# Layer 0 and 1 of a four-layer graph stack: when rows of adj are prepared, which comes first of roots, counts and fills, and how often adj is widened

## The reference, cut to what matters

```
L0:  deg = adj.T.sum(1); y = (d^-1/2 * adj.T * d^-1/2) @ (h @ W0) + b0
L1:  head = (adj > 0); head = head / max(sqrt(row sum of head^2), 1e-12)
     inc = adj + head; y = (inc @ h) / inc.sum(-1)
L2:  four heads: e = leaky_relu(src_i + dst_j) + adj; y = mean over heads of softmax(e) @ (h @ W2)
L3:  y = relu(adj @ (max(sign(h), 0) @ sign(W3).T))
```

## Time and profile before

| | us |
|---|---|
| median of three runs | 729.1 |
| the profiled execution | 732.13, span 730.2 |
| TensorE busy | 691.9 (95%) |
| VectorE busy | 629.2 (86%) |
| ScalarE busy | 480.3 (66%) |
| GpSimd busy | 106.9 (15%) |
| mean granted TensorE clock | 0.991 |

### The profile page before, as it was taken

The page is one execution under the profiler, slowest core; times in us unless marked ns, Lnnn a source line. Parts: engine busy times, 40 slices in busy tenths (PEclk is TensorE's granted clock), DMA queues, the critical chain, the costliest instruction groups (busy, mean ns, idle before and its releaser), DMA issues.

```text
span 730.2 us, 16136 instructions
## 1 busy us (share of the span) xinstructions
PE 691.9 (95%) x6480; PEld 585.0 (80%) x6480; DVE 629.2 (86%) x1165; ACT 480.3 (66%) x830; POOL 106.9 (15%) x146
## 2 busy tenths in 40 slices
PE   2898999996999999999999999999999899999998
PEld 2665888885888885458888888888888788888887
DVE  5887579788989864799999999989999799998683
ACT  3997162739987723886557867578766778667661
POOL 3002721211223220001210021200120100000000
PEclk9998999998999999999999999999999999999999
DMA  9886999868499976759988779897999931126791
GB/s 330 315 293 234 413 423 330 238 145 210 162 275 270 210 172 222 163 118 246 241 189 239 175 162 264 191 265 163 228 220 218 310 92 30 30 68 195 250 387 54
DMA packets 146458, 159.55 MB, mean 218 GB/s; under 512 B 90896, under 2 KB 103888, under 8 KB 141904
## 3 DMA queue, kind: packets, MB, share of 16 engines
q1 hardware_dynamic: 127328, 117.10, 54.4%
q0 software_dynamic: 19056, 41.42, 25.2%
HBM read 76.15 MB, written 52.46 MB: 176 GB/s over the span
## 4 chain that ended last, share of the span: by engine, by line
PE 55%; DVE 20%; ACT 10%; POOL 5%; issue 5%; DMA 4%; SPq 2%; ACTq 0%; POOLq 0%; DVEq 0%
PE ps L829 12%; PE ps L831 12%; PE ps L830 12%; PE ps L769 6%; DVE arena L1486 5%; DVE arena L1493 5%; PE ps L871 4%; PE ps L872 4%; ACT arena L1008 2%; ACT arena L1012 2%; DVE arena L1259 2%; DMA arena<-in_adj_dram 2%; DVE arena L1359 2%; POOL x L509 2%; SPq L384 2%
## 5 line engine op out<-in xcount | busy, mean ns | idle before, releaser
L829 PE MATMUL ps<-arena 128*128 128x257 f16 x1024 | 279.9, 273 | 2.9 <-DVE arena L1493 2.5
L831 PE MATMUL ps<-arena 128*128 128x257 f16 x1024 | 279.4, 273 | 0.0
L830 PE MATMUL ps<-arena 128*128 128x257 f16 x1024 | 279.2, 273 | 0.0
L1173 ACT ACTIVATE arena<-arena 128x512 f16<-128x512 f32 x252 | 158.5, 629 | 92.9 <-PE ps L831 55.1
L1486 DVE SCALAR_TENSOR_TENSOR arena<-arena,w_j 128x512 f32<-128x512 f32 x256 | 190.3, 744 | 0.0
L1493 DVE TENSOR_TENSOR arena<-arena 128x512 f16<-128x512 f32 x256 | 175.7, 687 | 10.3 <-ACT arena L1173 9.9
L829 PEld LDWEIGHTS ps<-arena 128*128 128x128 f16 x1024 | 99.9, 98 | 16.8 <-ACT arena L1173 4.1
L830 PEld LDWEIGHTS ps<-arena 128*128 128x128 f16 x1024 | 100.3, 98 | 12.5
L831 PEld LDWEIGHTS ps<-arena 128*128 128x128 f16 x1024 | 99.8, 97 | 13.0
L713 PE MATMUL ps<-arena 128*128 128x257 f16 x256 | 70.9, 277 | 1.6 <-DVE arena L1311 1.6
L715 PE MATMUL ps<-arena 128*128 128x257 f16 x256 | 70.2, 274 | 0.0
(11 more groups left out here) (155 smaller groups left out, 1110.9 us busy)
## 6 DMA issues: line engine op xcount, KB each, us to landing
adj_t<-arena POOLq DMA_DIRECT2D x32, 1024.0 KB, 7.9
arena<-in_adj_dram SPq DMA_DIRECT2D x32, 512.0 KB, 5.9
arena<-in_adj_dram SPq DMA_DIRECT2D x16, 1024.0 KB, 6.4
adj_parts<-arena SPq DMA_DIRECT2D x16, 1024.0 KB, 25.1
arena<-adj_t SPq DMA_DIRECT2D x64, 256.0 KB, 4.7
arena<-adj_t SPq DMA_DIRECT2D x16, 1024.0 KB, 6.9
x<-arena POOLq DMA_DIRECT2D x15, 512.0 KB, 5.8
arena<-u_rows SPq DMA_DIRECT2D x4, 1024.0 KB, 15.0
```

The costliest lines, as they stand in the source:

```text
L829: mm(ps[:, bank, 0:DE], hi, ht_hi[:, head, j, 0:DE], start=s, stop=False)
L830: mm(ps[:, bank, 0:DE], hi, ht_lo[:, head, j, 0:DE], start=False, stop=False)
L831: ins = mm(ps[:, bank, 0:DE], lo, ht_hi[:, head, j, 0:DE], start=False, stop=e)
L1173: nc.scalar.activation(p_hi[:, j % 4, :], prob[:, j % 4, :], copy).then_inc(p_hi_done, 1)
```

## The change

COUNTS, FILLS, HIGHS and LOWS get new iterations: seven rows instead of five are counted in layer 0, six instead of five filled, and all five splits end there, the fifth inc_low too. The buffers of rows are no longer t % 3: rows 0 to 3 share two buffers, and the third, in the bytes of nat's row 5, is used from row 4 on. SyncE's queue has its sends of nat in three portions with reloads and transposes between them. GpSimd takes the root of iteration t ahead of the count of iteration t - 1. In layer 1 VectorE's fill stands directly behind row_sums, ahead of all four part_low and the norm; fill 6 is in iteration 1, none in iteration 2, from iteration 3 fill t + 4 as before. ScalarE's signs and counts of layer 1 begin with row 7. WIDEN_AFTER names one group for each head from 0 to 9; widen groups 8, 9, 12 and 13 come one head sooner, the others at the head they had.

```diff
--- before.py
+++ after.py
@@ -186,14 +186,14 @@
         turn_l2 = [view(RING3 + off, [2, QB, TG * P], F16) for off in (8 * KB, 16 * KB)]
         adjt_early = [view(RING3 + 8 * KB * (k + 1), [N], F32) for k in range(2)]
 
-        COUNTS = (1, 2, 9, 10, 11)
-        FILLS = (3, 4, 11, 12, 14)
-        HIGHS = (4, 7, 12, 13, 15)
-        LOWS = (5, 8, 13, 14)
+        COUNTS = (1, 2, 6, 8, 10, 12, 14)
+        FILLS = (3, 4, 7, 9, 11, 13)
+        HIGHS = (4, 7, 9, 11, 13)
+        LOWS = (5, 8, 10, 12, 14)
         AHEAD = 5
         DMA_ROWS = ()
         PE_ROWS = [t for t in range(AHEAD, NB) if t not in DMA_ROWS]
-        WIDEN_AFTER = {0: (6,), 1: (7,), 3: (8,), 4: (9, 10), 5: (11,), 7: (12,), 8: (13, 14), 9: (15,)}
+        WIDEN_AFTER = {n - 6: (n,) for n in range(6, 16)}
         SENT = ((0, 1), (1, 3), (3, 5), (5, 8), (8, 11), (11, NB))
         EARLY = 4
         E_EARLY = 8
@@ -212,6 +212,15 @@
         H0_BANK = (0, 1, 6)
         DINV_PIECES = ((0, 1), (1, 4), (4, 9), (9, NB))
 
+
+        def inc_slot(t):
+            return t % 2 if t < 4 else (t - 2) % 3
+
+        def inc_use(t):
+            return sum(inc_slot(k) == inc_slot(t) for k in range(t + 1))
+
+        def inc_last(t):
+            return max(k for k in range(t) if inc_slot(k) == inc_slot(t))
 
         def row_slot(t):
             return 2 + (4 * t) // 3
@@ -363,10 +372,10 @@
 
 
             def load_rows(t):
-                sp.dma_start(rows[t % 3], adj_rows[t]).then_inc(rows_in[t % 3], 16)
+                sp.dma_start(rows[inc_slot(t)], adj_rows[t]).then_inc(rows_in[inc_slot(t)], 16)
 
             def reload_rows(t):
-                sp.wait_ge(filled, t - 2)
+                sp.wait_ge(filled, inc_last(t) + 1)
                 load_rows(t)
 
             def turn_inc(t):
@@ -390,20 +399,28 @@
                 load_rows(t)
             sp.wait_ge(h0_lo_done, NB)
             sp.dma_start(b0_bc, b0_d.partition_broadcast(P)).then_inc(bias_in, 16)
-            for k, (lo, hi) in enumerate(SENT):
+            def send_nat(k):
+                lo, hi = SENT[k]
                 for b in range(lo, hi):
                     sp.dma_start(nat_dram[b * P:(b + 1) * P], nat[:, b, :, :, :].rearrange("p a j n -> p a (j n)")
                                  ).then_inc(nat_sent[k], 16)
+
+            for k in range(4):
+                send_nat(k)
+            reload_rows(2)
             reload_rows(3)
-            reload_rows(4)
+            send_nat(4)
             sp.wait_ge(y_ps, 6)
             sp.wait_ge(max_made, 7)
             sp.wait_ge(nat_sent[3], 48)
-            load_rows(2)
+            load_rows(4)
             sp.wait_ge(nat_sent[2], 32)
             turn_inc(0)
+            send_nat(5)
+            reload_rows(5)
             sp.wait_ge(y_ps, 8)
             turn_inc(1)
+            reload_rows(6)
             sp.wait_ge(y_ps, 10)
             sp.wait_ge(max_made, 11)
             sp.wait_ge(nat_sent[4], 48)
@@ -412,10 +429,12 @@
                          ).then_inc(w2_in, 16)
             sp.wait_ge(nat_sent[5], 80)
             for t in range(2, AHEAD):
-                reload_rows(t + 3)
                 sp.wait_ge(y_ps, 10 + t)
+                sp.wait_ge(max_made, 11 + t)
                 turn_inc(t)
-            for t in range(AHEAD + 3, 12):
+                if t == 2:
+                    reload_rows(7)
+            for t in range(8, 12):
                 reload_rows(t)
             for k in range(5):
                 sp.wait_ge(nat_sent[k], 16 * (SENT[k][1] - SENT[k][0]))
@@ -545,12 +564,12 @@
 
             for t in range(NB):
                 inverse_root1(t)
-                if t in COUNTS:
-                    inverse_count(COUNTS.index(t))
+                if t - 1 in COUNTS:
+                    inverse_count(COUNTS.index(t - 1))
             for t in range(NB):
                 if t >= 1:
                     inverse_root2(t - 1)
-                if t + 5 < NB:
+                if 2 <= t and t + 5 < NB:
                     inverse_count(t + 5)
                 if t == 6:
                     widen_high(0)
@@ -998,14 +1017,14 @@
                                      ps[:, n % 3, :], copy, scale=ADJ_SCALE).then_inc(part_hi_done, 1)
 
             def sign(t):
-                act.wait_ge(rows_in[t % 3], 16 * (t // 3 + 1))
+                act.wait_ge(rows_in[inc_slot(t)], 16 * inc_use(t))
                 if t == 0:
                     act.wait_ge(y_ps, 1)
                     act.wait_ge(max_made, 2)
                     act.wait_ge(nat_sent[0], 16)
                 if t >= 2:
                     act.wait_ge(filled, t - 1)
-                nc.scalar.activation(mask[:, t % 2, :], rows[t % 3], ACT.Sign).then_inc(signed, 1)
+                nc.scalar.activation(mask[:, t % 2, :], rows[inc_slot(t)], ACT.Sign).then_inc(signed, 1)
 
             def count(t):
                 act.wait_ge(signed, t + 1)
@@ -1356,7 +1375,7 @@
                     dve.wait_ge(nat_sent[1], 32)
                 if t - 2 in PE_ROWS:
                     dve.wait_ge(t_ps, 4 * PE_ROWS.index(t - 2) + 4)
-                v.scalar_tensor_tensor(inc[:, t % 2, :], mask[:, t % 2, :], c_row[:, t:t + 1], rows[t % 3],
+                v.scalar_tensor_tensor(inc[:, t % 2, :], mask[:, t % 2, :], c_row[:, t:t + 1], rows[inc_slot(t)],
                                        ALU.mult, ALU.add).then_inc(filled, 1)
 
             def part_low(t, g):
@@ -1421,16 +1440,16 @@
                 more = t + 3 in PE_ROWS
                 if t >= 1:
                     row_sums(t - 1)
+                if t == 1:
+                    fill(6)
+                if 3 <= t and t + 4 < NB:
+                    fill(t + 4)
                 if more:
                     part_low(t + 3, 0)
                 if t >= 1:
                     row_norm(t - 1)
                 if more:
                     part_low(t + 3, 1)
-                if t == 0:
-                    inc_low(4)
-                if AHEAD <= t + 4 < NB:
-                    fill(t + 4)
                 if more:
                     part_low(t + 3, 2)
                     part_low(t + 3, 3)
```

## The result

The changed kernel takes 737.06 us (median of 4 runs), the kernel before 729.75 beside it: ratio 1.0087, 95% interval 1.0051 to 1.0123. It is slower by 7.3 us where I had forecast 1.2, and outside my range. The profiled executions have spans of 735.7 and 730.2, so they differ by 5.5: the profiled execution before took 732.13 us, 2.4 over its median, and the profiled one after 737.52, 0.5 over. One of the ten executions with the sends between took 1020 us at a granted clock of 0.66, and it is left out of that kernel's ratio.

A forecast was written before the change was run, and what follows sets the result against it. TensorE, busy nearly throughout, waits 10.2 us in layer 1 for VectorE's fill. Profiled 732.1 + 2.4 (up to row 15's transposes) - 1.2 (layer 2) = 733.3; +1.2 on the median gives 730.3 us, range 725.0 to 734.0.

The forecast's parts named there:

- The held sends: SyncE's queue, layer 0: holding back later nat sends costs nothing if transposes land in time; 0 to 3 us, taken 0.
- GpSimd's wait for the widening transfer: Layer 1: GpSimd's wait ahead of a root falls into the loop; 0.6 us taken, between 0 and 3.3.
- Layer 0's walk: VectorE's order in layer 0: period 11.8 us, last h1_low later, TensorE resumes at 166.6 instead of 164.07, +2.6 us.
- The closed loop: Layer 1: fill ahead of the norm makes each fill wait for its count; 8.3 us a row against TensorE's 7.46.
- The entry to layer 1: VectorE's first pass: row sums at 169.5, fill 6 from 170.1, part_low of row 5 at 176.9 against 175.55 before.
- The clock: TensorE's 4.1 us standstill before layer 1 lets the clock fall; 12 matmuls run at half rate, +1.3 us.
- Layer 2: Earlier widenings move transfers away from the exponentials' loads; -1.2 us taken, between -2.5 and 0.
- Removal wins: Rival, layer 1: the loop does not close and removing the fill stall makes it faster, 722.7 us; chance 0.20.
- Even trade: Rival: no second clock fall and the full 2.5 us of layer 2, 727.1, no change; chance 0.15.
- Held sends: Rival, SyncE's queue: row 1's transposes land late and delay the last h1_low; 733.3 us at upper price 3; chance 0.20.

The follow-up runs named there:

- sends between: Changed kernel with SyncE's queue reordered: sends of portions 0 to 4, reload of row 2, two sends, reload of row 3, last three sends; 732.9 us, ratio 1.0011.
- add_low 1 later: Changed kernel with add_low 1 in GpSimd's layer 1 order moved to iteration 9, behind that iteration's root and count; 734.0 us, ratio 1.0047.
- Counts two iterations ahead: Changed kernel with SyncE's sends reordered between reloads, plus counts taken two iterations ahead of their fill instead of one (new COUNTS, HIGHS); 729.2 us, ratio 0.9968.
- The norm ahead of the fill: Changed kernel with row_norm moved ahead of the fill in VectorE's layer 1 order, fill still ahead of all low parts; 736.8 us, ratio 1.0051.
- the fill back: Changed kernel with layer 1's fill back behind the second part_low, so behind the norm; 733.2 us, ratio 1.0008.
- roots first alone: Kernel before with only GpSimd's layer 0 order changed: root of iteration t ahead of the count of iteration t - 1; 726.7 us, ratio 0.9925.
- the new order alone: Kernel before with only the changed WIDEN_AFTER; 731.7 us, ratio 0.9993.
- the old order: Changed kernel with the old WIDEN_AFTER; 738.6 us, ratio 1.0089.
- all sends first: Changed kernel with all sixteen sends of nat first in SyncE's queue, ahead of the reloads of rows 2 and 3; 735.7 us, ratio 1.0051.

## Why the prediction was wrong, point by point

**The held sends: the step that failed.** I wrote that "the hold costs nothing if the transposes of rows 1 and 2 still land before inc_high 3 and 4 (142 and 154 in the walk)", had them land at 142 to 146 from the 18.3 us of the earlier trace rows, and set "Price from 0 to 3 us; I take 0". Row 1's had landed only when ScalarE went on at 150.98. The mechanism stood among the rivals, place and deciding point included; its size was wrong. The 18.3 us were not a rate: they held one pair of 13.3 us and one of 5.0, and my rival's "5 us a pair" is the second. In the changed kernel row 0's pair took 14.6 us with the five sends held behind it, and row 1's, behind these, 16.2 instead of 5.0. Price measured by the kernel with the sends between: 5.8 us at the last h1_low, 6.2 at row 5, 5.9 at row 15, 5.5 by the ratios, against a spread of row 5 from 174.0 to 179.1 in the five profiles without that edit and 168.84 with it.

**GpSimd's wait for the widening transfer: mis-sized.** "I take half, 0.6, between 0 and 3.3." It was 3.0 (add_low 1 later: 86.3 to 83.3 us). I took the slower rows to give the transfer time; instead it took 13.0 us (229.08 to 242.07) where before it had taken 10.6. Why it took longer is open.

**Layer 0's walk: right.** The waits for c_row (2.9 us once, 1.3 then), the period (11.7 for 11.8) and, with the queue repaired, the resumption (166.02 for 166.6) are as worked out. Counts two iterations ahead removed them, and all but 0.91 us of TensorE's standstill with them.

**The closed loop: right.** 8.3 us a row worked out, 8.36 measured, 8.47 in the rows with w2_a. The norm ahead of the fill removed the waits for c_row, the fill back gave rows of 7.46.

**The entry to layer 1: wrong, and hidden by luck.** I had the first row sums wait for 12 matmuls at the low clock, 2.9 us after the resumption. Row 0's last group waits for the last h1_low only with its last block, so three matmuls were left of it: with the sends between the sums start 0.54 us after the resumption, fill 6 at 167.17 (170.1 forecast) and the first part_low at 173.96 (176.9). That kernel starts row 15 at 255.4 where I had 255.5, but only because the 2.9 us that I had too many up to this part_low stood against as many too few behind it, GpSimd's wait above all.

**The clock: low as forecast, for a standstill that was another.** It was low at the resumption, in the changed kernel and with sends between, and behind the 3.71 us of roots first alone (0.50 over 170 to 172 us); with counts two ahead, where the standstill is 0.91 us, it stayed high. But I had one standstill of 4.1 us; with sends between there were two, of 0.83 and 2.04. And the 1.3 us that I charged for it were put ahead of the first row sums, where they weren't paid.

**Layer 2: -1.2 taken, -2.7 seen, and not for my reason alone.** The heads last 346.2 us before, 344.7 with the new order alone, 344.7 in the changed kernel with the old order, 343.5 changed, and 343.5 with roots first and the old order; in the other kernels, all with the new order, 342.6 to 343.9. The widening order is worth 1.2 and 1.5 us in the two pairs that differ in nothing else and isn't told from nothing in time; what gives the rest, I have not shown.

**The rivals.** Removal wins: false, the loop closed. Even trade: false, the clock fell. Held sends: true, at nearly twice its upper price, and beside the forecast's own terms rather than in their place. In the profiles the sum closes like this: row 15 was forecast 2.4 us late and without the queue's fault is 2.3 late (255.4), by the luck above; the sends add 5.9, layer 2 gives back 2.7, which makes the 5.5 between the spans. In time, too, the kernel with the sends between is where the forecast was: ratio 1.0011, 0.8 us slower than the kernel before for a forecast of 1.2. The 7.3 between the medians are 1.9 more than the spans' 5.5, since the profiled execution of the kernel before was 2.4 us over its median and the changed kernel's 0.5.

## What to carry to other kernels

When an instruction is moved ahead on an in-order engine, follow what stood between its old place and its new one: if the moved instruction waits for something that the passed ones release, a loop closes, and its length, added up from start to start over all engines, is the new row time. A send that a queue holds back costs nothing by itself, until a transfer that is needed soon stands behind it; price each such transfer by a row of its own, since one merged row hid 13.3 and 5.0 us in its 18.3. And a pair of "sooner" edits can each be right and still need a third: here the earlier counts, which take the latency out of the fills.

## What the runs showed of the hardware

A load of 1 MB that left SyncE's queue behind sixteen sends of 1 MB at 99.63 had landed when the sign behind it started at 118.68, 19.0 us later (all sends first; the median of such loads there is 6.0). Two DMA transposes of 512 KB each held SyncE's queue for 4.6 us (152.24 in the kernel before) up to 16.7 (110.02, all sends first), and what was issued after them left the queue only behind them (124.59 in the changed kernel). Row 1's pair took 16.2 us behind five sends and a load in the changed kernel, 8.8 with the sends moved ahead, 5.0 in the kernel before; row 0's, which follows queued sends in each of the three, took 14.6, 16.3 and 13.3. That the bytes ahead are what slows a pair is my reading of this order. The granted clock fell also without one long standstill: with sends between, TensorE stood 0.83 and 2.04 us with a few matmuls between, and ran at 1.2 GHz for most of 166 to 168 (stretches of that kernel; PEclk is the last but two):

```profile
164.00:166.00 2.00, 0.00 (x0) 0.00 (x0) 0.90 (x3) 1.21 (x4) 1.35 (x3) 1.00 1.13 208
166.00:168.00 2.00, 1.98 (x12) 1.48 (x13) 1.40 (x3) 1.25 (x1) 0.00 (x0) 0.61 1.38 231
```
